# Rows of a fused convolution and mixture kernel turned by VectorE instead of TensorE, with a low part made by GpSimd

## What is computed

```python
K = 2.0 * jnp.einsum('hn,hnl->hl', Cs, jnp.exp(P)).real        # one row of 1024 per head
y = jnp.fft.irfft(u_f * k_f, n=n)[..., :Lq]                    # u = x masked by length
y = y + u_m * D[:, None]
x = x + y * mask[:, None, :]
```

```python
base = jnp.einsum('btd,od->bto', x, W)
logits = jnp.einsum('btd,ed->bte', x, Wr) + bias               # top 2, softmax -> gates
h = jnp.einsum('btd,erd->bter', x, A)
x = x + base + 2.0 * jnp.einsum('bter,bte,eor->bto', h, gates, B)
```

## Time and profile before

| | |
|---|---|
| runs of the kernel | 664.57, 664.79, 667.07 us |
| the profiled execution | 665.17 us, of which 663.4 us are its span |
| TensorE clock granted, mean | 0.992 |
| TensorE busy | 641.9 us, 97% of the span |
| VectorE busy | 491.8 us, 74% |
| ScalarE busy | 462.5 us, 70% |
| GpSimd busy | 35.1 us, 5% |
| DMA queue of SyncE / of ScalarE | 17.9% / 9.6% of 16 engines' span |

### The profile page before, as it was taken

How to read it: one execution, slowest core, us unless ns; L and a number is a source line. 1 busy time by engine, 2 the same in 40 slices (tenths; PEclk the granted TensorE clock), 3 DMA queues, 4 the chain that set the end, 5 groups by cost and what they waited for, 6 DMA issues and landing times.

```text
span 663.4 us, 12421 instructions
## 1 busy us (share of the span) xinstructions
PE 641.9 (97%) x3663; PEld 616.3 (93%) x3663; DVE 491.8 (74%) x1504; ACT 462.5 (70%) x977; POOL 35.1 (5%) x61
## 2 busy tenths in 40 slices
PE   4798999999999999999999999999999999999997
PEld 4697989999999999999999999999999999999997
DVE  7888687777778777777877777787777778776741
ACT  5788788586776858686686868678676867864531
POOL 2241000000000000000000000000000000000000
PEclk9798999999999999999999999999999999999999
DMA  6531313333312132322213223211333321122212
GB/s 186 151 104 32 82 39 66 72 71 71 68 36 59 50 71 71 71 71 46 57 40 71 71 71 71 59 45 39 71 71 71 71 67 39 42 66 41 41 33 63
DMA packets 24064, 43.40 MB, mean 65 GB/s; under 512 B 9928, under 2 KB 14832, under 8 KB 24048
## 3 DMA queue, kind: packets, MB, share of 16 engines
q1 hardware_dynamic: 19168, 27.37, 17.9%
q10 hardware_dynamic: 4880, 15.83, 9.6%
HBM read 26.35 MB, written 16.85 MB: 65 GB/s over the span
## 4 chain that ended last, share of the span: by engine, by line
PE 91%; ACT 4%; DVE 3%; issue 1%; DMA 0%; ACTq 0%; SPq 0%; DVEq 0%
PE pmg L1269 58%; PE pc L1208 13%; PE pmg L1256 7%; PE px L1208 5%; PE px L1201 4%; PE pmg L1250 1%; DVE state L935 1%; PE pmg L1279 1%; PE pmg L1167 1%; ACT swapped L531 1%; PE pmg L1177 1%; DVE w_lo L867 0%; DMA logs<-in_L_cond_log_A_real 0%; ACT y_hi L558 0%; ACT z_swap L480 0%
## 5 line engine op out<-in xcount | busy, mean ns | idle before, releaser
L1269 PE MATMUL pmg<-w_hi,y_hi 128*128 128x384 f32 (+1 forms) x768 | 265.7, 346 | 0.7 <-DVE y_lo L982 0.7
L1269 PE MATMUL pmg<-w_hi,y_lo 128*128 128x384 f32 (+1 forms) x768 | 259.8, 338 | 0.0
L1269 PE MATMUL pmg<-w_lo,y_hi 128*128 128x384 f32 (+1 forms) x768 | 259.7, 338 | 0.0
L1269 PEld LDWEIGHTS pmg<-w_hi,y_hi 128*128 128x128 f32 x768 | 144.3, 188 | 1.7 <-issue 1.1
L1269 PEld LDWEIGHTS pmg<-w_hi,y_lo 128*128 128x128 f32 x768 | 144.4, 188 | 0.5
L1269 PEld LDWEIGHTS pmg<-w_lo,y_hi 128*128 128x128 f32 x768 | 144.3, 188 | 0.0
L531 ACT ACTIVATE swapped<-state 64x128 f32<-64x128 f32 x192 | 59.4, 309 | 65.4 <-DVE state L935 64.0
L935 DVE SCALAR_TENSOR_TENSOR state<-swapped,scan_tab,state 128x192 f32<-128x192 f32 (+1 forms) x240 | 73.8, 349 | 15.6 <-ACT swapped L531 11.1
L576 ACT ACTIVATE result<-pmg 128x384 f32<-128x384 f32 (+1 forms) x96 | 41.7, 448 | 39.4 <-PE pmg L1256 37.1
L964 DVE TENSOR_TENSOR s_lo<-state,s_hi 128x896 fp32r<-128x896 f32 x31 | 33.9, 1093 | 30.0 <-ACT s_hi L553 30.0
L982 DVE TENSOR_TENSOR y_lo<-xt,y_hi 128x1024 fp32r<-128x1024 f32 x32 | 39.2, 1225 | 20.6 <-ACT y_hi L558 19.2
(11 more groups left out here) (206 smaller groups left out, 1112.0 us busy)
## 6 DMA issues: line engine op xcount, KB each, us to landing
rows<-in_x SPq DMA_DIRECT2D x64, 256.0 KB, 5.3
out<-result ACTq DMA_DIRECT2D x60, 256.0 KB, 4.0
toe<-kpad SPq DMA_DIRECT2D x30, 128.0 KB, 5.1
rows<-in_L_cond_W SPq DMA_DIRECT2D x3, 512.0 KB, 6.9
result<-in_L_cond_W SPq DMA_DIRECT2D x3, 512.0 KB, 5.9
w_rows<-in_L_cond_W SPq DMA_DIRECT2D x2, 512.0 KB, 4.5
result<-in_L_cond_A SPq DMA_DIRECT2D x1, 512.0 KB, 6.2
b_rows<-in_L_cond_B SPq DMA_DIRECT2D x2, 256.0 KB, 6.7
```

The costliest lines, as they stand in the source:

```text
L1269: ins = nc.tensor.matmul(pm[:, n, 0:o1 - o0], y[s][:, c, :], w[:, c, o0:o1], start=(c == 0 and y is y_hi and w is w_hi), stop=(c == CH - 1 ...
```

## The change

Three things are changed, for the pairs from 4 on.

The rows are loaded as blocks: eight transfers for a pair (`load_blocks`), each of 32 partitions times 16 pieces of 32 floats (128 bytes). A partition of `rows` then holds 32 samples of a chunk for every chunk, head and sequence of its 32x32 squares, so that turning each square on its own gives `xt`.

VectorE turns the squares, two instructions of 128x512 for a pair (`turn_rows` in the VectorE block), from `rows` straight into `xt` in SBUF. TensorE's eight transposes and ScalarE's copy of `px` into `xt` go, and ScalarE's `u_hi` is now made from `xt`.

GpSimd makes `u_lo` (`low_rows`). On VectorE `s_lo` moves from the end of a step to behind `route` of the next one, and in the m = 0 steps `zo_lo` (`split_obs`) moves behind `split_gated`. TensorE's `control` now has the two waits for the `px` banks that `turn_rows` had, and SyncE's wait for a free `rows` tile is for VectorE's turn (`xt_ready`) instead of TensorE's (`px_full`).

```diff
+            def load_blocks(b, m):
+                i, s = 2 * b + m, m % 2
+                for k in range(P // SQUARE):
+                    for d in range(SEQS // SQUARE):
+                        sp.dma_start(
+                            rows[s][k * SQUARE:(k + 1) * SQUARE, d * HALF:(d + 1) * HALF].rearrange(
+                                "p (n l) -> p n l", l=SQUARE),
+                            bass.AP(x.tensor, 2 * i * LEN + k * SQUARE + d * (SQUARE * HEADS * LEN),
+                                    [[HEADS * LEN, SQUARE], [P, 2 * CH], [1, SQUARE]])
+                        ).then_inc(rows_in[s], 16)
...
             def step(b, m, rows_left=True):          # SyncE
                 if rows_left:
-                    sp.wait_ge(px_full, 2 * b + m + 3)
-                    load_rows(b, m + 4)
+                    sp.wait_ge(xt_ready, 2 * b + m + 3)
+                    load_blocks(b, m + 4)
                 store_kernel(b, m + 3)
                 load_toe(b, m + 3)
...
+            def low_rows(b, m):                      # GpSimd
+                s = m % 2
+                pool.wait_ge(uhi_ready, 2 * b + m + 1)
+                vec.tensor_tensor(u_lo[s][:, :, :], xt[s][:, :, :], u_hi[s][:, :, :].bitcast(F32), ALU.subtract
+                                  ).then_inc(ulo_ready, 1)
             with pool.Fori(1, LOOPS) as b:
                 pool.wait_ge(z2_ready, b + 2)
                 stage_gen(b + 2)
                 pool.wait_ge(scan, SCAN * (2 * b + 2))
                 stage_scan(b + 1)
+                for m in range(2):
+                    low_rows(b, m + 2)
...
+            def split_turned(b, m):                  # ScalarE, in the place of split_rows
+                i, s = 2 * b + m, m % 2
+                act.wait_ge(xt_ready, i + 1)
+                act.wait_ge(conv_done, i - 1)
+                nc.scalar.activation(u_hi[s][:, :, :], xt[s][:, :, :], ACT.Copy).then_inc(uhi_ready, 1)
...
+            def turn_rows(b, m):                     # VectorE
+                i, s = 2 * b + m, m % 2
+                dve.wait_ge(rows_in[s], TURNED_BY_PE + BLOCK_LOADS * (b + m // 2 - 1))
+                dve.wait_ge(ylo_ready, i - 1)
+                for d in range(SEQS // SQUARE):
+                    turned = xt[s][:, :, :].rearrange("p c (h d b) -> p h c d b", h=2, b=SQUARE)[:, :, :, d, :]
+                    blocks = rows[s][:, d * HALF:(d + 1) * HALF].rearrange("p (h c l) -> p h c l", h=2, l=SQUARE)
+                    ins = vec.transpose(turned, blocks)
+                ins.then_inc(xt_ready, 1)
...
                 if rows_left:                        # VectorE's step
                     split_ctr(b, m + 2)
-                    split_obs(b, m + 2)
+                    if m == 1:
+                        split_obs(b, m + 2)
                 if kernels and m == 1:
                     powers(b + 2)
                 route(b, m)
-                if rows_left:
-                    split_rows(b, m + 2)
+                split_states(b, m + 1)
+                split_gated(b, m)
+                if rows_left and m == 0:
+                    split_obs(b, m + 2)
                 if kernels and m == 0:
                     angles(b + 2)
-                split_gated(b, m)
                 merge(b, m + 1)
...
                     for _ in scan_states(b, m + 2):
                         pass
-                    split_states(b, m + 2)
+                if ahead:
+                    turn_rows(b, m + 3)
...
-            def control(b, m):                       # TensorE
-                i, s = 2 * b + m, m % 2
+            def control(b, m, alone=False):
+                i, s = 2 * b + m, m % 2
+                if alone:
+                    pe.wait_ge(v_copied, i)
+                    pe.wait_ge(scan, SCAN * (i - 1) + 1)
...
                 if rows_left:
-                    control(b, m + 2)
-                project(b, m, 2, 0, 7)
-                if ahead:
-                    turn_rows(b, m + 3)
-                project(b, m, 2, 7, 8)
+                    control(b, m + 2, alone=True)
+                project(b, m, 2)
                 add_lora(BANK_ORDER[2])
```

More of the change, by code:

```diff
@@ L37 @@
 DUOS = HEADS // DUO
+SQUARE, HALF = 32, LEN // 2
 MAGIC = 1.5 * 2.0 ** 23
@@ L237, in cond_resid_kernel @@
         START = 16
+        TURNED_BY_PE = 64
+        BLOCK_LOADS = 16 * 8
         ROUTER = 9
@@ L334, in _ @@
             sp.wait_ge(px_full, 3)
-            load_rows(0, 4)
+            load_blocks(0, 4)
             sp.wait_ge(pm_free, 6)
@@ L344, in step @@
                 if rows_left:
-                    sp.wait_ge(px_full, 2 * b + m + 3)
-                    load_rows(b, m + 4)
+                    sp.wait_ge(xt_ready, 2 * b + m + 3)
+                    load_blocks(b, m + 4)
                 store_kernel(b, m + 3)
                 load_toe(b, m + 3)
-            step(0, 1)
+            sp.wait_ge(px_full, 4)
+            load_blocks(0, 5)
+            step(0, 1, rows_left=False)
             with sp.Fori(1, LOOPS) as b:
@@ L430, in _ @@
                 stage_scan(b + 1)
+                for m in range(2):
+                    low_rows(b, m + 2)
             pool.wait_ge(scan, SCAN * (2 * LOOPS + 2))
             stage_scan(LOOPS + 1)
+            for m in range(2):
+                low_rows(LOOPS, m + 2)
         def scan_scalar(k, j, h, staged):
@@ L692, in step @@
                 if rows_left:
-                    split_rows(b, m + 2)
+                    split_turned(b, m + 2)
                 ratios(b, m)
@@ L1104, in _, with step @@
                 pass
-            split_states(0, 3)
-            def step(b, m, rows_left=True, kernels=True):
+            turn_rows(0, 4)
+            def step(b, m, rows_left=True, kernels=True, ahead=True):
                 split_toe(b, m + 1)
@@ L1133, in _ @@
             step(LOOPS, 0, kernels=False)
-            step(LOOPS, 1, kernels=False)
-            step(LOOPS + 1, 0, rows_left=False, kernels=False)
+            step(LOOPS, 1, kernels=False, ahead=False)
+            step(LOOPS + 1, 0, rows_left=False, kernels=False, ahead=False)
             route(LOOPS + 1, 1)
@@ L1364, in _, with step @@
             add_lora(BANK_ORDER[2])
-            turn_rows(0, 4)
-            def step(b, m, rows_left=True, ahead=True):
+            def step(b, m, rows_left=True):
                 if rows_left:
@@ L1387, in _ @@
             step(LOOPS, 0)
-            step(LOOPS, 1, ahead=False)
-            step(LOOPS + 1, 0, rows_left=False, ahead=False)
+            step(LOOPS, 1)
+            step(LOOPS + 1, 0, rows_left=False)
             wait_y(LOOPS + 1, 1)
```

## The result

The changed kernel takes 685.69 us (median of 4 runs, 684.79 to 686.32). The kernel before, run beside it, takes 665.93 us (4 runs, 664.57 to 667.87). The ratio is 1.0295, 95% interval 1.0272 to 1.0319: 3% slower, 19.8 us. The forecast was 673 us. It was right in sign and in the main mechanism, GpSimd's `u_lo` holding VectorE up, and wrong in size and in the place of the stop in m = 1 steps.

What follows compares the result with a forecast made beforehand. TensorE bounds, 97% busy, in a near-slackless ring with VectorE. With `u_lo` blocking VectorE, periods of 19.53 and 19.49 sum to 39.02 against 38.47 us, adding 7.7 to 665.17: 672.9, said as 673 us; own range 668 to 680, overall 641 to 690.

Steps and rivals of the forecast that it cites:

- the ring: Loop of TensorE and VectorE: turn of the gates, convolution, merge, scan, route, `gated`, next turn; 38.47 us for two steps before.
- S: The end of a scan on VectorE, the zero from which the forecast counts times within a step.
- The rival without blocking: Tiny instructions such as `weight` are not blocked beside GpSimd: two steps in 36.91 us, 643 us in all; chance 0.32.
- VectorE reaches `weight`: VectorE in route: two-input `weight` is what waits for GpSimd, ready at S + 4.15 (m = 0) and S + 4.61 (m = 1).
- lets go at S + 5.65: m = 1 step: GpSimd's `u_lo` runs S + 3.50 to S + 5.88 and frees VectorE at S + 5.65.
- the way from S to the end of `gated`: VectorE from scan end through route to `gated`: 6.35 us (m = 1) and 5.88 us (m = 0) before the change.
- the way from the turn to the end of the scan: From a turn of the gates on TensorE to the next scan's end: 12.65 and 12.81 us, left unchanged.
- the wider lock: GpSimd holds the ports to its end and also blocks casts and instructions with a constant: 690 us, chance 0.10.
- a lock that is held for a whole instruction: The port pair shared by VectorE and GpSimd is exclusive to whoever starts first, until that instruction ends.
- The 0.23 us: How long before GpSimd's end a blocked VectorE instruction seemed to start, from the prologue's `zo_lo` at 43.38.

Runs made afterwards that it cites:

- E7: E1 with `s_lo` back at the end of its own step, behind the transposes, instead of behind `route` of the next: 660.84 us, ratio 0.9935.
- E4: The kernel before with only the 128-byte block loads, TensorE turning the tile as before (output differs): 664.97 us, ratio 0.9998.
- E1: The changed kernel with `u_lo` back on VectorE behind `s_lo`, and `zo_lo` ahead of `route` in both parities: 645.33 us, ratio 0.9691.
- E2: The kernel before with only `u_lo` moved to GpSimd, for pairs from 4 on: 711.15 us, ratio 1.069.
- E5: E1, but in m = 1 steps GpSimd makes `u_lo` and waits for `s_lo` first: 643.44 us, ratio 0.967.
- E8: The changed kernel with the two-element cast `top_no` split into two one-element casts: 679.47 us, ratio 1.0223.
- E3: The changed kernel with the `top_no` cast split in two and `weight` made a tensor_scalar with a pointer: 675.81 us, ratio 1.0167.
- E9: The changed kernel with GpSimd's subtraction replaced by a 128x1 subtraction and two TENSOR_SCALAR instructions from `xt` (output differs): 668.65 us, ratio 1.0056.
- E6: The changed kernel with GpSimd's subtraction replaced by a 128x1 subtraction and two copies of `xt` (output differs): 655.54 us, ratio 0.9844.

## Why the prediction missed

**Right.** TensorE's relief counts only as far as the ring gets shorter: E7 shows it, with 3.3 us of 24.4. The transposes took 1.30 us for two, as forecast, and lie in the wait for `t_hi`; `t_lo` started at S + 1.34 in m = 1 (314.37 less 313.03; forecast S + 1.37). Loads and their issues are hidden (E4; and in the changed kernel VectorE waits for no transfer of `rows`). GpSimd's `u_lo` stops a one-element `weight` in m = 0, shown by E1 and E2 to be the cause. The rival without blocking put 643 us on a kernel in which nothing stops; E1 and E5, in which nothing of `route` stops, measure 645 and 643.

**Wrong.** The step that failed is "VectorE reaches `weight`" as the place of the stop in m = 1, and with it "lets go at S + 5.65", that is 0.23 us before GpSimd's end. The cast ahead of `weight` stopped, until GpSimd's end, and the way from S to the end of `gated` took 7.18 us instead of 6.74. Besides, the way from the turn to the end of the scan, which the forecast left as it was, grew by 0.28 us in one parity. Measured for two steps against the forecast:

| term | forecast | measured | difference |
|---|---|---|---|
| turn to end of scan, m = 0 turn | 12.65 | 313.03 - 300.10 = 12.93 | 0.28 |
| turn to end of scan, m = 1 turn | 12.81 | 333.17 - 320.34 = 12.83 | 0.02 |
| S to end of `gated`, m = 1 | 6.74 | 320.21 - 313.03 = 7.18 | 0.44 |
| S to end of `gated`, m = 0 | 6.62 | 339.91 - 333.17 = 6.74 | 0.12 |
| `gated` to the turn, twice | 0.20 | 0.26 | 0.06 |
| sum | 39.02 | 39.94 | 0.92 |

14 times 0.92 are 12.9 us, and 672.9 + 12.9 = 685.8 us; the profiled execution took 685.87.

- The 0.44 us: the cast stops, GpSimd holds it to its end (S + 5.79), and from there `half_sum` and its reciprocal still come ahead of `weight`, which starts at S + 6.10 (319.13) and not at S + 5.65. GpSimd itself was 0.09 us earlier than forecast: it started at 316.42, and `powers`, which was to keep it waiting, ended at 316.46. E8 splits the cast, which then passes, and regains 0.46 us for two steps.
- The 0.12 us: `weight` was forecast to end at S + 5.70 (5.54 + 0.16) and ends at S + 5.82, 0.02 us behind GpSimd.
- The 0.28 us: I took the way from turn to scan as fixed. Before, the m = 0 turn's matmul stood in a stream, and the convolution's first one started 0.03 us behind it; at the m = 1 turn, taken 0.14 us after `gated`, it started 0.23 us behind (the turns are those of the earlier trace rows):

```profile
292.40 0.48 PE L1208 MATMUL pc<-u_hi,t_hi 128*128 128x512 f32 x1
...
311.74 0.47 PE L1208 MATMUL pc<-u_hi,t_hi 128*128 128x512 f32 x1
```

Now TensorE comes to both turns from a standstill, and the convolution starts 0.33 us behind (300.10, 300.43) and 0.24 us behind (320.34, 320.58). The differences, 0.30 and 0.01, are the 0.28 and 0.02 of the table within 0.02. So a wait ahead of the turn also cost what the two matmuls had overlapped. No run isolates this term; it is read from the rows.

The rival that I gave 0.10, the wider lock at 690 us, was the nearer account: held to the end, casts stopped. It was too wide in one point, since `half_sum` and other one-input instructions of one element pass (E3, E8), and its release at GpSimd's end stands in place of the forecast's 0.23 us before it. I had put it low because no row showed a blocked cast; but I had read none of a cast passing beside GpSimd either. The Trainium skill names copies and casts, when their operands let them into the modes with two ports, among the contenders (SBUF — State Buffer, "Who interferes with whom"). The traces agree for a cast of two elements (1.68 us instead of 0.17). One of one element passed (0.15 us beside GpSimd in E8); no run shows in which mode either ran. The prediction also told of a lock that is held for a whole instruction. GpSimd's subtraction and copy fit that; its TENSOR_SCALAR in E9, which let VectorE in after 0.95 us, does not.

The 0.23 us were read from one row, taking the mean of 0.51 us as the length of the blocked instruction. That mean has the blocked row itself, of 1.55 us, in it; the median of the 32 is 0.48, which makes it 0.20 us. In the loop, a blocked instruction of 0.16 us ends 0.02 us after GpSimd: it looks as if part of an instruction's time is behind it already when it is let go. No run tests that.

## What to carry to other kernels

When work goes to GpSimd, look at what VectorE does at that time and not at how busy either is. One subtraction of 2.4 us in each of 28 steps cost 46 us in the kernel before and 40 us here; in 14 steps, behind `s_lo`, where VectorE waits anyway, it cost nothing that the times show. Find the first instruction on VectorE of a form that stops, count from GpSimd's end everything that still follows it up to the waiting engine, and remember that relief of the busiest engine pays only as far as the ring through the others gets shorter.

## What the runs showed of the hardware

- While GpSimd's subtraction in SBUF runs, VectorE stops, until it ends, at: a product of two SBUF tensors even of one element (1.90 us instead of 0.16), a cast of two elements (1.68 instead of 0.17), a tensor_scalar with pointers of eight (1.77 in the m = 0 steps of E3, instead of 0.28). The first two stop at GpSimd's copy too (0.78 and 0.59 in E6). It does not stop at a cast of one element (0.15), a tensor_scalar of one element (0.21), or the search for the maxima of 128x8 and their places (0.16 each, from 316.63 on in the changed kernel, behind GpSimd's start at 316.42).
- GpSimd's TENSOR_SCALAR of 128x896 (2.45 us) lets VectorE in after 0.95 us and can stop it again later (E9); a copy of the same size takes 0.94 us and held a VectorE instruction that came 0.37 us into it to its end (E6).
- VectorE turns 32x32 squares of float32 at 0.69 us for 128x512, 1.30 us for two in a row.

```profile
L923 DVE STREAM_TRANSPOSE xt<-rows 128x512 f32<-128x512 f32 x56 | 36.3, 687 | 0.0
```

- 4096 pieces of 128 bytes for a pair, in place of 128 of 4 KB, cost SyncE 4.1 to 6.5 us of issue (E4, seven pairs from 280 to 420 us) instead of 1.2 to 1.3, and no time of the kernel (ratio 0.9998, E4).
